# A two-layer attention and expert kernel on one core: first-layer keys spread by 16 transfers, scores first in a step, and ScalarE normalising the second layer's input rows

## The reference

```python
# layer 0: queries from the tokens, keys and values from the context
q = layernorm(x) @ Wq + bq ; k = ctx @ Wk + bk ; v = ctx @ Wv + bv      # 16 heads of 8
x = x + tanh(g_xattn[0]) * (softmax(q k^T / sqrt(8)) v @ Wo + bo)
x = x + tanh(g_ffn[0]) * experts_top2_of_8(layernorm(x))                 # routed
# layer 1: the same 8x8 weights for every head, softmax over energy / sqrt(128)
x = x + tanh(g_xattn[1]) * (softmax(masked(q1 k1^T)) v1 @ Wo1.T + bo1)
x = x + tanh(g_ffn[1]) * experts_dense_4(x)                              # depth gated
```

## Time and profile before

| | us |
|---|---|
| median of 3 runs | 1396.92 |
| the profiled execution's own time | 1402.06 |
| its span in the trace | 1400.3 |
| TensorE busy | 1155.6 |
| VectorE busy | 900.4 |
| ScalarE busy | 752.5 |
| GpSimd busy | 541.8 |

### The profile page before, as it was taken

How to read it: one execution, slowest core, us unless ns; L and a number is a source line. 1 busy time by engine, 2 the same in 40 slices (tenths; PEclk the granted TensorE clock), 3 DMA queues, 4 the chain that set the end, 5 groups by cost and what they waited for, 6 DMA issues and landing times.

```text
span 1400.3 us, 40016 instructions
## 1 busy us (share of the span) xinstructions
PE 1155.6 (83%) x13845; PEld 947.0 (68%) x13845; DVE 900.4 (64%) x3061; ACT 752.5 (54%) x1629; POOL 541.8 (39%) x699
## 2 busy tenths in 40 slices
PE   6887778876785399999996777778777778899998
PEld 3665555655564199999995455556555556799997
DVE  4776655665565654555552377667667677998887
ACT  4876566665563055555552466555555566444443
POOL 2114443435535544444444444454444333122220
PEclk9999888988887699999998699899889899999999
DMA  6222111111100233333322111111111110000000
GB/s 184 77 79 67 57 38 41 45 33 43 49 26 31 68 95 94 94 94 94 94 72 76 32 35 34 37 36 35 35 35 34 33 31 4 9 23 22 22 22 23
DMA packets 116780, 71.89 MB, mean 51 GB/s; under 512 B 51736, under 2 KB 105240, under 8 KB 116632
## 3 DMA queue, kind: packets, MB, share of 16 engines
q1 hardware_dynamic: 108440, 53.13, 14.0%
q0 software_dynamic: 8192, 16.79, 4.0%
HBM read 45.88 MB, written 22.94 MB: 49 GB/s over the span
## 4 chain that ended last, share of the span: by engine, by line
PE 52%; issue 15%; DVE 12%; another core or an unknown queue 11%; ACT 5%; SPq 3%; POOL 2%; DMA 1%; DVEq 0%; ACTq 0%; POOLq 0%
PE ps_m L1759 9%; PE ps_p L1519 4%; PE ps_p L1644 4%; PE ps_m L1644 4%; PE ps_s L1476 3%; DVE mx L982 3%; PE ps_s L1745 3%; PE ps_s L1486 3%; PE ps_s L1746 2%; PE ps_s L1747 2%; PE ps_p L1534 2%; PE ps_s L1633 2%; PE ps_s L1632 2%; PE ps_s L1634 2%
## 5 line engine op out<-in xcount | busy, mean ns | idle before, releaser
L982 DVE TENSOR_REDUCE mx<-ps_s 128x8 f32<-128x512 f32 x256 | 170.3, 684 | 161.3 <-remote 112.8
L713 ACT ACTIVATE PT<-ps_p 128x512 f32<-128x512 f32 x320 | 188.2, 599 | 100.5 <-remote 41.3
L585 POOL TENSOR_TENSOR ve<-mv,eps 128x4 f32<-128x4 f32 x72 | 14.9, 207 | 439.8 <-DVE mv L925 439.8
L1519 PE MATMUL ps_p<-cst,Pr 128*128 128x128 f32 x1024 | 165.5, 297 | 13.7 <-issue 10.8
L797 ACT ACTIVATE Kbd<-ps_s,c 128x512 f32<-128x512 f32 x128 | 87.3, 688 | 113.4 <-PE ps_s L1634 113.4
L1519 PEld LDWEIGHTS ps_p<-cst,Pr 128*128 128x128 f32 x1024 | 134.5, 156 | 19.0 <-issue 17.2
L652 POOL DMA_INDIRECT w1a<-louts,gi x128 | 124.9, 976 | 38.6 <-issue 29.7
L1759 PE MATMUL ps_m<-xn3T 128*128 128x128 f32 x1136 | 137.9, 275 | 0.0
L576 POOL TENSOR_TENSOR spare<-spare 1x1 f32<-1x1 f32 x99 | 21.3, 215 | 290.4 <-DVE b1s L1337 151.1
L1759 PEld LDWEIGHTS ps_m<-xn3T 128*128 128x128 f32 x1136 | 132.7, 192 | 0.0
L863 ACT ACTIVATE xn3T<-ps_s,b1s 128x256 f32<-128x256 f32 x284 | 111.3, 475 | 26.1 <-PE ps_s L1747 26.1
(11 more groups left out here) (221 smaller groups left out, 2855.5 us busy)
## 6 DMA issues: line engine op xcount, KB each, us to landing
xn3T<-lists SPq DMA_DIRECT2D x71, 128.0 KB, 2.1
louts<-xn3T SPq DMA_DIRECT2D x71, 128.0 KB, 1.8
ctxg<-in_ctxT SPq DMA_DIRECT2D x32, 256.0 KB
Kbd<-in_ctxT SPq DMA_DIRECT2D x512, 8.0 KB
out<-x SPq DMA_DIRECT2D x16, 256.0 KB, 2.3
w1a<-in_L_ffn_W SPq DMA_DIRECT2D x8, 256.0 KB
w2a<-in_L_ffn_W SPq DMA_DIRECT2D x8, 256.0 KB
Pr<-in_ctxT SPq DMA_DIRECT2D x16, 128.0 KB, 2.5
```

The source lines that it names most:

```text
L713: return nc.scalar.activation(dst, src, ACT.Copy)
L982: V.tensor_reduce(mx[g.par][:, q, :], per_key(ps_s[:, q, :]), AX, ALU.max).then_inc(max_done, 1)
L1519: ins = turn(ps_p[:, c % 2, P * i:P * i + P], Pr[g.par][:, j // 2, col:col + P], ident)
```

## The change

Layer 0's keys are made two groups ahead. PE's `keys(g + 2)` writes only the keys; ACT copies them once, with their bias, into one buffer `kT`; SP's `spread_keys` then moves them into `Kbd` with one transfer of 8 partitions for each of the 16 heads, 10 ahead of the context load and 6 behind it. POOL fills both `Kbd` buffers with zeros at the start. The mask columns are gone. The context is loaded three groups ahead, from step -1 on. `queries(g + 1)` stands alone. Values move from bank 3 of `ps_s` to the second bank of `ps_m`.

PE now begins each step with `scores`, in both layers. The order of banks is 0, 2, 3, 1: VectorE takes the maximum of bank 0 and subtracts it first, then banks 2 and 3, then bank 1. ACT's order follows: the exponential of bank 0 and the queries stand early in the step, the exponential of bank 1 and the sums late. In layer 1 DVE no longer normalises the rows for the queries: it computes -mean * rs for two tiles (`shift_in`), and ACT applies scale and bias (`normalise_in`). Below, `keys`, `normalise_in` and the first run of `now` calls are ACT's, the second run is PE's for layer 0.

```diff
-ORDER = (2, 3, 0, 1)
+ORDER = (0, 2, 3, 1)
...
+            def spread_keys(g, some):
+                if 0 in some:
+                    if g.k == 0:
+                        sp.wait_ge(kbd_clear, 1)
+                    sp.wait_ge(k_ready, g.count(1, 1))
+                    wait(sp, s_done, g.count(4, -4))
+                for h in some:
+                    rows = slice(DK * h, DK * h + DK)
+                    sp.dma_start(Kbd[g.par][rows, :, h % 4, :],
+                                 kT[rows, :].rearrange("p (b k) -> p b k", b=4)).then_inc(spread_in[g.par], 16)
...
             def step(g):
-                if g.plus(2).real() and (g.layer or g.k >= 0):
+                if g.layer == 0:
+                    if g.plus(2).real():
+                        spread_keys(g.plus(2), range(0, 10))
+                    if g.plus(3).real() and g.k >= -1:
+                        load_ctx(g.plus(3))
+                    if g.plus(2).real():
+                        spread_keys(g.plus(2), range(10, H))
+                elif g.plus(2).real():
                     load_ctx(g.plus(2))
...
+            nc.gpsimd.memset(Kbd[0][:, :, :, :], 0.0)
+            nc.gpsimd.memset(Kbd[1][:, :, :, :], 0.0).then_inc(kbd_clear, 1)
...
+            def keys(g):
+                act.wait_ge(k_done, g.count(1, 1))
+                if g.k:
+                    act.wait_ge(spread_in[1 - g.par], 16 * H * ((g.k - 1) // 2 + 1))
+                copy(kT[:, :], kq_bank[:, 0:GT], bcol[:, 1:2]).then_inc(k_ready, 1)
...
+            def normalise_in(g):
+                act.wait_ge(nb_ready, g.at(1, 1))
+                wait(act, xt_done, g.count(1, -1))
+                for j in range(2):
+                    nc.scalar.activation(xn[g.par][:, j, :], x[:, 2 * g.k + j, :], ACT.Identity, bias=nb[:, j:j + 1],
+                                         scale=rs[:, 2 + j:3 + j]).then_inc(xn_ready, 1)
...
                 now(probs_out, -1, 1)
-                now(tokens2, -3)
+                now(exps, 0, 0)
+                now(queries, 1)
+                if g.layer == 0:
+                    now(keys, 2)
                 now(probs_out, -1, 2)
                 if g.layer == 1:
                     now(values, 0)
-                now(probs_out, -1, 3)
                 now(exps, 0, 2)
                 now(exps, 0, 3)
+                now(probs_out, -1, 3)
+                now(tokens2, -3)
+                now(exps, 0, 1)
+                now(sums_out, -1)
...
+                    now(scores, 0)
                     now(probs_turned, -1, 0)
                     now(tokens_turned, 1)
                     now(heads_turned, -2)
                     now(probs_turned, -1, 1)
-                    now(scores, 0)
+                    now(keys, 2)
+                    now(queries, 1)
+                    now(project_out, -2)
+                    now(probs_turned, -1, 2)
+                    now(less_maximum, 0, 2)
+                    now(less_maximum, 0, 3)
+                    now(probs_turned, -1, 3)
                     now(tokens2_turned, -3)
...
                     now(values_by_probs, -1)
-                    now(keys_queries, 1)
+                    now(values, 1)
```

122 lines of the change are left out of this document (55 added, 67 removed).

## The result

The changed kernel takes 1538.33 us (median of 4 runs, 1527.72 to 1540.05) against 1399.53 us (4 runs) of the kernel before: a ratio of 1.0995, 95% interval 1.0947 to 1.1042. The forecast was 1381 and faster. It is 139 us slower, 125 above the upper end of the range.

A forecast was written before the change was run, and what follows sets the result against it. No engine full: a TensorE-VectorE chain bounds clean steps, a loop through POOL's indirect transfers and late TensorE results the others. Start +20.3, clean steps -13, scatter steps -29, second layer +6: -15.7, median 1381 us; 8-in-10 range 1346 to 1413.

The forecast's parts named there:

- The price of an issue: SP's 16 spread transfers in each first-layer step: 0.35 us per issue, 5.66 us together, taken from the second layer's transfers.
- the landing: First-layer spread transfers: the last lands 1.4 us after its issue, bounds 0.9 to 2.5.
- my loop: First layer, key copy to next key copy through SP's issues, context load and landing: 8.2 us, shorter than a step.
- The start: First layer: the spread waits behind SP's prologue, first scores at about 37.5, +20.3 us (bounds +19.5 and +23).
- Clean steps of 9.3: First-layer steps without scatters: scores first shortens them from 10.93 to 9.3 us, -13 us over 8 steps (0 to -16).
- Scatter steps of 12.5: First-layer steps with scatters: next scores start inside the scatters, 12.46 against a mean 14.08, -29 us (0 to -60).
- Rival 1: First layer: late results still caught every second step, scatter steps keep 14.08; +13, 1410 us; chance 0.15.
- The second layer: Second-layer steps: POOL's loop hides ScalarE's longer path, so the step stays near 12.9; +6 us (-10 to +43).
- rival 2: Second layer: gathers catch the later sums, steps of 14.5; two of three 29 us, total 1405, all 1419; chance 0.12.
- the gathers' loop of 12.7: Second layer: scores visible, VectorE, POOL's four gathers, TensorE's late results; 12.7 us against a mean step of 12.86.
- Rivals 3 and 4: Rival 3, first layer: spread transfers lengthen the scatters' delay, 22 us, total +6, 1403; chance 0.11. Rival 4: own line.
- Rival 4: First-layer scatter steps: TensorE only loses about 2.1 us, steps of 11.4, 59 gained instead of 29, 1351; chance 0.15.

The follow-up runs named there:

- late sets: Sets of runs where the kernel before takes 1380 to 1400 us and TensorE's results come late beside indirect transfers; the changed kernel's first set had ratio 1.0995.
- prompt set: Set of runs without those late results: the kernel before, unchanged, takes 1186.47 us; the changed kernel, unchanged, 1364.4 us, ratio 1.150.

## Why the prediction was wrong

- **The price of an issue** failed. I took 0.35 us from the second layer's transfers "of the same shape", and bounded only the landing. It is 0.73, as it is for every SBUF source tried; the second layer reads DRAM rows 64 KB apart. This is one term; my loop with it gives 14.2, the trace 14.14, against a step of 9.3 to 12.5 that I thought would cover it. In late sets it carries 27 to 33 us of the 27 steps (414.0 and 420.8 against 387.3 with half of the transfers), in a prompt set 108 (384.8 against 277.2), and about 20 of the start (102.3 against 82.5 for the fifth scores). The landing, on which the prediction spent its bounds and a rule of the Trainium skill, was right: 1.28 measured, 1.4 taken. The page "DMA: Bandwidth & Descriptors" of the Trainium skill (section "Anatomy of one DMA") says, of transfers issued from GpSimd, that completion, not setup, makes up the fixed cost; the prediction applied it to SP's without saying so. For one of SP's transfers here that is so (1.28 against 0.69). For sixteen in one queue it is not: 11.6 us of issues, one landing.
- **The start**: the mechanism (SP's prologue) was right, and the first scores near 37.5 came true where the issues together take what I had put for them (37.7 with eight slow ones, 36.4 with sixteen fast ones); in the changed kernel it is 42.0. What I missed is that a load in front holds whatever is behind it, and that the key product, two groups ahead, waits for a context load there too.
- **Clean steps of 9.3** came true as soon as SP let them: 9.0 to 9.3. But there are fewer of them than I counted: every fourth step, and near the end every second, carries the router's ranks and takes 11.5 to 12.9. I had read one step and multiplied.
- **Scatter steps of 12.5** failed twice: SP's loop, and the wait for the logits' read, which I had listed in no part. It comes after the scatters by the very delay I had described (1.17 us after the last one's record). In a late set 27 steps stay 35 us above the old order without SP's bound (387.3 against 352.1), where -37 was forecast; that this wait makes them is read from one kind of step and not isolated. Rival 1 (the pairing stays) is what is left of it, at more than its price: the steps got longer, not equal.
- **The second layer** failed in the choice between forecast and rival 2. The sum of ScalarE's path (sums at 7.2, next scores at 8.0) was nearly right (7.23 and 8.2 in the prompt trace), and I let the gathers' loop of 12.7 hide it. They don't hide each other fully: +34.9 us, between rival 2's two prices (29 and about 44), though not by even steps of 14.5 as it has them: the steps range from 9.9 to 19.8. Its chance, 0.12, was too small. The gathers begin 6.8 us after the results by the earlier trace rows and not 6.65 as rival 2 says, which changes nothing. The normalisation, which I put into ScalarE's idle time at 0.38 us a tile, takes 0.485 and costs nothing, as I had it.
- **Rivals 3 and 4**: traffic of this kind beside the scatters is worth at most 10 us; and nothing here came out faster. Rival 4 (a length, not an end) has no support: where results are late, they come 1.06 to 1.17 us after the last scatter's record.
- **The range** failed because the issue price, a number that the trace of before did not show for this source, had no upper bound of its own. With 0.73 as a bound, SP's loop of 14.2 us a step would have stood in it.

## What to carry to other kernels

Price a queue of small transfers by the issue time of the very source and destination, not of a like shape; and write the engine that issues as a row of the step's budget, with everything that stands behind. Before putting one piece of work first in a step, list every wait in its head, the rare ones too (each fourth step's ranks), and ask when each comes in the slowest kind of step. Relief of an engine counts only for steps in which it is the last to be ready.

## What the hardware showed

- Issuing a transfer of 8 rows of 1 KB from SP takes 0.30 us with DRAM source rows 64 KB apart, 0.65 to 0.66 with DRAM rows 1 KB apart, and 0.67 to 0.74 from SBUF, in one piece or four a row, into SBUF in each case.
- The same program with the same data takes about 1185 us or 1380 to 1400 in different sets of runs, on the same chip. In the second kind results of TensorE are late while indirect transfers run; POOL's own 958 ns a transfer are the same.
- The first transfer that SP issues behind the load of x (3.7 MB) holds its queue for 9.4 to 13.2 us, whether it is a mask, a spread transfer, a context load or a store; no load of another size was tried.
- A store of 128 KB from SBUF to DRAM lands 3.65 us after its issue ends; a spread transfer within SBUF 1.28 us after its own.
